# Low parts of the second and third masked pair: minus the high part from ScalarE and an accumulating transfer, in place of VectorE's difference

## The reference

```
top_p, top_i = top_k(softmax(gelu(xf @ w_r1 + b_r1) @ w_r2 + b_r2), 2); top_p /= sum(top_p)
for _ in range(2):
    ctx = concat(integrated, v)                                  # (2048, 256)
    shared_ctrl = gelu(ctx @ w_s1 + b_s1) @ w_s2 + b_s2
    x_shared, v_shared = inl(shared_ctrl, integrated, v, mu)
    hidden = gelu(ctx_e @ expert_w1[top_i] + expert_b1[top_i])   # 64 per chosen expert
    ctrl = hidden @ expert_w2[top_i] + expert_b2[top_i]          # 3 * 128: alpha, beta, gate
    x_r, v_r = weighted sum over the two experts of inl(ctrl, x_e, v_e, mu)
    x_next, v_next = sw * x_shared + (1 - sw) * x_r, sw * v_shared + (1 - sw) * v_r
    halt = sigmoid(gelu(x_next @ w_h1 + b_h1) @ w_h2 + b_h2)
    refined = gelu(x_next @ w_f1 + b_f1) @ w_f2 + b_f2
    integrated, v = integrated + halt * refined * integration_weight, v_next
```

## Time and profile before

| | |
|---|---|
| median of three runs | 358.88 us |
| the profiled execution | 360.02 us |
| its span | 358.2 us, 4385 instructions |
| TensorE | 327.9 us busy (92%), 1513 matmuls |
| VectorE | 284.2 us (79%) |
| ScalarE | 196.2 us (55%) |
| GpSimd | 21.1 us (6%) |
| chain that ended last | 70% TensorE, 19% VectorE, 3% ScalarE, 3% GpSimd, 2% DMA, 4% issue |

### The profile page before, as it was taken

How to read it: one execution, slowest core, us unless ns; L and a number is a source line. 1 busy time by engine, 2 the same in 40 slices (tenths; PEclk the granted TensorE clock), 3 DMA queues, 4 the chain that set the end, 5 groups by cost and what they waited for, 6 DMA issues and landing times.

```text
span 358.2 us, 4385 instructions
## 1 busy us (share of the span) xinstructions
PE 327.9 (92%) x1513; PEld 231.5 (65%) x1521; DVE 284.2 (79%) x598; ACT 196.2 (55%) x309; POOL 21.1 (6%) x24
## 2 busy tenths in 40 slices
PE   4989999899888889599798999999999999999996
PEld 4754787445454557367476677777777777777663
DVE  0556767655768777979997999999997997999694
ACT  2500025385637285186876686775855846734744
POOL 0040020202010112000000100000000000000000
PEclk9989999999999999789899999999999999999999
DMA  7999920000000000000000010100100100000001
GB/s 248 425 424 298 333 124 0 0 4 0 0 0 2 1 0 2 0 0 3 1 0 2 5 24 0 31 0 2 30 0 3 29 0 2 29 0 0 31 0 59
DMA packets 11445, 18.92 MB, mean 53 GB/s; under 512 B 416, under 2 KB 8864, under 8 KB 10144
## 3 DMA queue, kind: packets, MB, share of 16 engines
q1 hardware_dynamic: 10848, 17.60, 14.3%
q0 software_dynamic: 576, 1.05, 1.7%
HBM read 16.55 MB, written 1.05 MB: 49 GB/s over the span
## 4 chain that ended last, share of the span: by engine, by line
PE 70%; DVE 19%; issue 4%; ACT 3%; POOL 3%; DMA 2%; SPq 0%; DVEq 0%; ACTq 0%; POOLq 0%
PE ps L1200 65%; DVE zz L803 4%; POOL lrs L359 3%; DVE lst L788 2%; DMA ctxT<-in_ctxT 2%; PE ps L1297 1%; PE ps L1383 1%; PE ps L1276 1%; DVE lmv L791 1%; DVE st L688 1%; ACT hid L484 1%; PE ps L1371 1%; DVE a L704 1%; DVE lve L793 1%; DVE ctxT L1090 0%
## 5 line engine op out<-in xcount | busy, mean ns | idle before, releaser
L1200 PE MATMUL ps<-hm_odd,ew_hi 128*128 128x512 f32 (+1 forms) x164 | 52.3, 421 | 0.0
L1200 PE MATMUL ps<-hm_even,ew_hi 128*128 128x512 f32 (+1 forms) x160 | 49.7, 414 | 0.0
L1200 PEld LDWEIGHTS ps<-hm_odd,ew_hi 128*128 128x128 f32 (+1 forms) x164 | 29.1, 191 | 6.5 <-issue 0.5
L1200 PEld LDWEIGHTS ps<-hm_even,ew_hi 128*128 128x128 f32 (+1 forms) x160 | 27.5, 188 | 5.2
L1200 PE MATMUL ps<-hm_odd,ew_lo 128*128 128x512 f32 (+1 forms) x80 | 28.8, 397 | 0.0
L1200 PE MATMUL ps<-hm_even,ew_lo 128*128 128x512 f32 (+1 forms) x80 | 28.0, 390 | 0.0
L484 ACT ACTIVATE hid<-ps,pB 128x512 f32<-128x512 f32 x32 | 21.7, 687 | 10.4 <-PE ps L1200 9.7
L1200 PE MATMUL ps<-x_hi,w1x_hi 128*128 128x512 f32 x40 | 20.1, 503 | 5.7 <-ACT hid L484 3.9
L803 DVE TENSOR_SCALAR zz<-ps,lmv,lrs 128x128 f32<-128x128 f32 x48 | 16.4, 405 | 7.7 <-POOL lrs L359 7.5
L897 DVE SCALAR_TENSOR_TENSOR ring<-ring,pB,hid 128x1024 f32<-128x1024 bf16 x16 | 20.5, 1283 | 0.9
L788 DVE BATCH_NORM_STATS2 lst<-ps 128x6 f32<-128x128 f32 x48 | 10.7, 285 | 11.9 <-PE ps L1276 11.8
(11 more groups left out here) (286 smaller groups left out, 740.0 us busy)
## 6 DMA issues: line engine op xcount, KB each, us to landing
ring<-in_fc1b SPq DMA_DIRECT2D x4, 1024.0 KB, 17.8
ring<-in_fc2a SPq DMA_DIRECT2D x4, 1024.0 KB, 9.0
packC<-in_packC SPq DMA_DIRECT2D x1, 1152.0 KB, 9.2
pB<-in_packB SPq DMA_DIRECT2D x1, 1141.5 KB, 10.1
ctxT<-in_ctxT SPq DMA_DIRECT2D x2, 512.0 KB, 6.6
xtok<-in_xtok SPq DMA_DIRECT2D x1, 1024.0 KB, 9.2
xT<-in_xT SPq DMA_DIRECT2D x1, 1024.0 KB, 11.2
a<-in_fc1a SPq DMA_DIRECT2D x1, 1024.0 KB, 13.2
```

The source lines that it names most:

```text
L1200: return pe.matmul(out, lhsT, rhs, start=start, stop=stop)
```

## The change

VectorE keeps the masks and the high parts of all pairs, and the low part of tile 0 and of pair 1. For pairs 2 and 3, ScalarE writes minus `hm` to the low half, which as an fp32r value is minus the high part (`negative_high`), and GpSimd issues a transfer that adds `hm` to it in place (`low_part`, 512 KB). The semaphores `nhi` (ScalarE's copy) and `hlo_2`, `hlo_3` (the transfers) are new; the next masks wait on the transfers where they waited on the difference. In the BETA groups the three matmuls of each tile of pairs 2 and 3 are split in order: first high parts, at the end low parts. GpSimd's two loops are merged into one sequence.

```diff
             for n in range(3 * NCH):
+                power(n)
+            low_part(0, 2)
+            low_part(0, 3)
+            for s in range(1, STEPS):
+                if 3 <= s < NCH + 3:
+                    residual(s - 3)
+                low_part(s, 2)
+                low_part(s, 3)
...
+            def low_part(s, j):
+                pool.wait_ge(sem("nhi"), 2 * s + j - 1)
+                if s >= 1:
+                    pool.wait_ge(sem(f"hlo_{j}"), 16 * s)
+                pool.dma_start(low_of(s, j), hm[j % 2], accum_op=ALU.add).then_inc(sem(f"hlo_{j}"), 16)
...
+            def negative_high(s, j):
+                act.wait_ge(sem("hm"), (HT - 1) * s + j)
+                act.activation(low_of(s, j), hm[j % 2], ACT.Copy, scale=-1.0).then_inc(sem("nhi"), 1)
...
+            negative_high(0, 2)
+            negative_high(0, 3)
             act.wait_ge(sem("consts"), 4)
             for s in range(STEPS):
...
                 if s >= 1:
                     halt1(s - 1)
+                if s + 1 < STEPS:
+                    negative_high(s + 1, 2)
+                    negative_high(s + 1, 3)
                 squashed(s, parts(s)[1])
...
@@ kept(s, j)
-                if s >= 1 or j == 3:
-                    dve.wait_ge(sem("hlo"), HT * s + (0, -1, 2)[j - 1])
+                    if s >= 2:
+                        dve.wait_ge(sem("part_ps"), group(s - 1, 0))
+                if j == 3:
+                    dve.wait_ge(sem("hlo"), 2 * s + 2)
+                elif s >= 1:
+                    dve.wait_ge(sem("hlo_2" if j == 2 else "hlo_3"), 16 * s)
...
@@ hidden_masked(s, next_state)
                 lower(s, 0)
+                high(s, 1)
                 lower(s, 1)
                 kept(s, 3)
-                lower(s, 2)
+                high(s, 2)
                 shared_halves(s)
-                lower(s, 3)
+                high(s, 3)
...
@@ controls
-                    pe.wait_ge(sem("hlo"), HT * s + j + 1)
-                    out = hi if k else lo
-                    mm(out, weights(ew2_hi, j), m[:, 0, i, :], start=rows_last and j == 1, stop=False)
-                    mm(out, weights(ew2_lo, j), m[:, 0, i, :], start=False, stop=False)
-                    last = mm(out, weights(ew2_hi, j), m[:, 1, i, :], start=False,
-                              stop=not rows_last and j == HT - 1)
+                    high(i)
+                    if not rows_last or i < 3:
+                        last = low(i)
+                if rows_last:
+                    for i in range(3, NT):
+                        low(i)
```

More of the change, by code:

```diff
@@ L302, in masked, with high_of, low_of @@
             return hm_odd if s % 2 else hm_even
+        def high_of(s, j):
+            return masked(s)[:, 0, 2 * j - 1:2 * j + 1, :]
+        def low_of(s, j):
+            return masked(s)[:, 1, 2 * j - 1:2 * j + 1, :]
         SLOTS = NCH + 2
@@ L355, in _, with power @@
             pool.wait_ge(sem("r1one"), 1)
-            for n in range(3 * NCH):
+            def power(n):
                 pool.wait_ge(sem("lve"), n + 1)
@@ L360, in _, with residual @@
                     .then_inc(sem("lrs"), 1)
-            for s in range(NCH):
+            def low_part(s, j):
[3 more added lines that the diff above has]
+                pool.dma_start(low_of(s, j), hm[j % 2], accum_op=ALU.add).then_inc(sem(f"hlo_{j}"), 16)
+            def residual(s):
                 pool.wait_ge(sem("xi"), s + 1)
                 pool.dma_start(xT[:, ck(s)], xi[:, ck(s)], accum_op=ALU.add).then_inc(sem(f"xsum_{s}"), 16)
+            for n in range(3 * NCH):
+                power(n)
[6 more added lines that the diff above has]
+                low_part(s, 3)
         @block.scalar
@@ L473, in hidden_gelus @@
                         if s >= 1:
-                            act.wait_ge(sem("hm") if j else sem("hlo"), (HT - 1) * (s - 1) + j if j else HT * (s - 1) + 1)
+                            act.wait_ge(sem("hm") if j else sem("hlo"), (HT - 1) * (s - 1) + j if j else 2 * s - 1)
                         if j == 0:
@@ L899, in kept, with high @@
                                          ALU.is_equal, ALU.mult).then_inc(sem("hm"), 1)
+            def high(s, j):
+                dve.wait_ge(sem("hm"), (HT - 1) * s + j)
+                dve.tensor_copy(high_of(s, j), hm[j % 2]).then_inc(sem("hhi"), 1)
             def lower(s, j):
@@ L906, in lower @@
                     dve.wait_ge(sem("hhi_0"), s + 1)
[L907 to L915, removed]
+                    dve.tensor_tensor(out[:, 1, 0, :], hid[:, 0, :], out[:, 0, 0, :].bitcast(F), ALU.subtract)\
                         .then_inc(sem("hlo"), 1)
                 else:
-                    dve.tensor_tensor(out[:, 1, 0, :], hid[:, 0, :], out[:, 0, 0, :].bitcast(F), ALU.subtract)\
+                    dve.wait_ge(sem("hhi"), (HT - 1) * s + 1)
+                    dve.tensor_tensor(low_of(s, 1), hm[1], high_of(s, 1).bitcast(F), ALU.subtract)\
                         .then_inc(sem("hlo"), 1)
@@ L1053, in _ @@
             kept(0, 2)
+            high(0, 1)
             lower(0, 1)
@@ L1056, in _ @@
             state_split(1)
-            lower(0, 2)
+            high(0, 2)
             shared_halves(0)
-            lower(0, 3)
+            high(0, 3)
             route(NCH - 1)
@@ L1525, in weights, with high, low @@
                     return w[:, j * 3 * D + part * D:j * 3 * D + (part + 1) * D]
+                def high(i):
+                    j, k = TILES[i]
+                    pe.wait_ge(sem("hhi"), (HT - 1) * s + j)
+                    mm((lo, hi)[k], weights(ew2_hi, j), m[:, 0, i, :], start=rows_last and j == 1, stop=False)
+                    mm((lo, hi)[k], weights(ew2_lo, j), m[:, 0, i, :], start=False, stop=False)
+                def low(i):
+                    j, k = TILES[i]
+                    if j == 1:
+                        pe.wait_ge(sem("hlo"), 2 * s + 2)
+                    else:
+                        pe.wait_ge(sem(f"hlo_{j}"), 16 * (s + 1))
+                    last = mm((lo, hi)[k], weights(ew2_hi, j), m[:, 1, i, :], start=False,
+                              stop=not rows_last and j == HT - 1)
+                    if n == LAST and j == HT - 1:
+                        last.then_inc(sem("stream_ps"), 1)
+                    return last
                 def shared(first):
@@ L1536, in row_tiles @@
                     pe.wait_ge(sem("hsl"), s + 1)
-                    pe.wait_ge(sem("hlo"), HT * s + 1)
+                    pe.wait_ge(sem("hlo"), 2 * s + 1)
                     w_hi, w_lo = weights(ew2_hi, 0), weights(ew2_lo, 0)
@@ L1556, in controls @@
                 for i in (1, 3, 5, 2, 4, 6) if n == LAST else range(1, NT):
-                    j, k = TILES[i]
                     if i == 4 and between:
                         between()
-                    pe.wait_ge(sem("hlo"), HT * s + j + 1)
-                    out = hi if k else lo
-                    mm(out, weights(ew2_hi, j), m[:, 0, i, :], start=rows_last and j == 1, stop=False)
-                    mm(out, weights(ew2_lo, j), m[:, 0, i, :], start=False, stop=False)
-                    last = mm(out, weights(ew2_hi, j), m[:, 1, i, :], start=False,
-                              stop=not rows_last and j == HT - 1)
-                    if n == LAST and j == HT - 1:
-                        last.then_inc(sem("stream_ps"), 1)
+                    high(i)
[4 more added lines that the diff above has]
+                        low(i)
                 if rows_last:
```

## The result

The changed kernel takes 364.23 us (median of 4 runs, 363.83 to 364.61) where the kernel before takes 359.34 beside it (4 runs, 358.85 to 359.83). The ratio is 1.0136, 95% interval [1.0114, 1.0158]: slower by 4.9 us. The forecast was 362.5 in a range of 360.2 to 365.2, from a delay of 3.6.

The account below looks back on a forecast made before the run. TensorE was taken to bound the kernel from 197.6 to 331.7 us, with earlier waits on ScalarE's gelus. +1.80 + 2.76 - 0.94 = +3.6 us on the median 358.88 gave 362.5 us, range 360.2 to 365.2.

Parts of the forecast that it names:

- The bound: From 197.6 to 331.7 us TensorE is busy 134.07 of 134.10 us; time off VectorE there buys nothing by itself.
- Price of a copy, and the places: A 128x1024 ScalarE copy costs 0.95 us; between last gelu and GATE's tanh calls, delay reaches TensorE in four places.
- Step 0: Two copies ahead of the table load delay GATE's tanh, the gelu and TensorE's `hidden(2)` by 1.80 us.
- `hidden(3)`: TensorE's wait for ScalarE's gelu, 1.28 us, comes 0.92 later with the copies, to about 2.2.
- `hidden(4)` and `hidden(5)`: Copies behind the halt gelu delay GATE's tanh by 0.92 us each; TensorE's waits there come to about 1.1.
- The end: Step 7: without two VectorE subtractions, TensorE's wait before `refine_a(6)` goes whole, -0.94 us.
- The order, GpSimd and the transfers: BETA low parts last, sixteen GpSimd issues, 512 KB transfers landing in 5.1 us: all covered, no cost.
- the rival on late landings: Step 0's transfers at 7.4 us each in series make TensorE wait 2.9 us: 365.4 and above; chance 0.07.
- The clock: Rival: a second clock fall, behind the 2.2 us wait in `hidden(3)`, adds 1.6 us: 364.1; chance 0.20.
- The first fall: Behind the `hidden(2)` wait the clock fell to 0.53 for 3.3 us, about 1.6 lost; no change counted.
- The sum: Step 0, steps 1 to 3 and the end: +1.80 + 2.76 - 0.94 = +3.6 us.
- its two terms: Top of the range, 365.2: clock fall, +1.6 us, and dear copies at 1.02 each, +0.6, together.

Follow-up runs that it names:

- Steps 1 to 3 alone: Copies and transfers only for the masks of steps 2 to 4, copied in ScalarE's steps 1 to 3, against the kernel before: 362.30 us, 1.0075.
- Split places: Whole change, one copy ahead of the halt gelus and one behind, step 0's both ahead of the weights' copies, against the kernel before: 358.98 us, 0.9989.
- second part alone: Copies and transfers only for the masks of steps 5 to 7, the others by VectorE's difference, against the kernel before: 358.16 us, 0.9973.
- order: All differences on VectorE, only the change's order of BETA matmuls and its mask waits, against the kernel before: 358.93 us, 0.9990.
- step 0 alone: Copies and transfers only for the masks of step 1, copied in ScalarE's step 0, against the kernel before: 361.97 us, 1.0066.
- first part alone: Copies and transfers only for the masks of steps 0 to 4, VectorE's difference for 5 to 7, against the kernel before: 364.77 us, 1.0166.
- filler: Extra matmuls into a free bank at the start of the `hidden(2)` wait: ten in the kernel before, 0.9978; eighteen in the change, 1.0099 to the kernel before.

## Why the prediction was right, and which term was short

- **The bound.** TensorE sets the pace from 197 us on, and time off VectorE buys nothing there: right. Without any of the differences of six steps the kernel gains 1.2 us, all but a little of it the one wait at the end.
- **Price of a copy, and the places.** 0.95 us from start to start was forecast and measured. Step 0 in the trace: +1.79 for 1.80. `hidden(3)`: +0.88 for 0.92. `hidden(4)` and `hidden(5)`: +0.81 and +0.83, and waits of 0.77 where 1.1 was forecast. There the tanh did move by 0.90, but some 0.1 came back right behind it: L484 used to start 2.15 us after the tanh, now 2.04. The gelu ahead of it (L482) started at 215.63 in the trace of before, 0.04 after the end of the last matmul that it needs; the copies have moved it well behind that. Steps 1 to 3 alone cost 2.7 us on the clock of the runs, with 2.76 forecast. Split places shows that the mechanism is the place and not the copy.
- **The end.** -0.94 forecast; -0.97 in the traces, and -0.97 with the second part alone. That L1097 waits next for the tanh, and that this still leaves the whole wait, held.
- **The order, GpSimd and the transfers.** Priced at nothing, and no TensorE wait ends on a transfer: right within the intervals (order 0.9990; transfers at most 0.0017). The landings are 4.5 to 6.7 us: the pair-2 ones near the 5.1 taken, those of pair 3, which start 0.9 us behind, 6.1 and 6.2 (median). That is past the 5.9 from which the rival on late landings was to decide, but that rival had the two in series at 7.4 each; they run side by side and land within 8 us of the first issue. One statement here was wrong: "The new waits of `kept` on the transfers are met 5 us or more ahead". In step 1 the mask on VectorE waits 2.31 us for the pair-3 transfer of step 0, up to 157.48. No cost of it shows: TensorE works from 155.66 on without a gap.
- **The clock.** This is the term that was shown to be short, for 0.6 of the 1.3 us missing, in the rival's sentence "The first fall may also come out shorter, as more of it is spent waiting; I count nothing". It came out longer: 6.7 us low instead of 3.4. Step 0's copies cost 2.4 us instead of 1.80, and the traces of the change and of step 0 alone gain 0.5 behind the wait, where the clock is low. The size is not fixed: in the first part alone the same wait of 4.43 gives a shorter fall, with 16.9 us where the change has 17.5. The rival itself, a second fall behind the 2.2 us wait, came in one of the five traces that have that wait, the one of steps 1 to 3 alone, and cost 1.4 there; that the prediction left it out of its sum and gave it a chance was sound. Its price of 1.6 a fall doesn't follow from its own count: nine matmuls instead of fourteen, at 0.23 each, are some 1.2 us, and the traces give 1.3. What holds in place of "I count nothing": a delay that lengthens an idle stretch of the array is to be priced with the fall behind it, at either size, and as a thing that comes in some executions only.
- **The sum.** +2.4, +2.7 and -0.97 make 4.1 of the 4.9 measured, forecast 3.6. The other 0.8 isn't settled. It has the size by which the first part alone exceeds its two halves, and lies within the intervals. A second fall of 1.4 us in some of the executions could give as much, but the one trace of the change has none, and no run tests it.

The measured delay of 4.9 lies nearer to the 5.2 of the clock's rival than to the 3.6 of the forecast; the mechanism of the forecast carries most of it, and the rest is that rival's kind of cost in part and open in part. The range's top of 365.2 is 0.5 above what its two terms give (362.5 + 1.6 + 0.6 = 364.7); the measured 364.23 lies below both. And the forecast in time, 362.5 for 364.23, is off by 0.5 more than that in the delay, as the kernel before, 358.88 in the first three runs, was 359.34 beside the changed one.

## What to carry to other kernels

Before moving work to an engine with idle time, look up in its timeline what stands behind the place and who waits for that: with the sixteen copies at one place the kernel lost 4.9 us, and with half of the copies put ahead of the two instructions that stood before them it lost nothing. Look for the gap of the right size on each side of the instructions that others wait for, and put there what fits. A relief counts only where the relieved engine is waited for, so the change is worth making for three steps of eight at most (0.9973).

## What the runs showed of the hardware

**GpSimd's issue of a transfer can be held by a VectorE cast.** In the trace of after, GpSimd's first two issues of the low parts, the third, and the casts of VectorE beside the first two:

```profile
149.70 1.35 POOL L375 DMA_DIRECT2D hm_even<-wz  x1 [6.34 <-ACT hm_even L569]
150.63 1.86 POOL L375 DMA_DIRECT2D hm_even<-ring  x1
169.77 0.87 POOL L375 DMA_DIRECT2D hm_odd<-wz  x1 [17.28 <-ACT hm_odd L569]
```

```profile
150.19 0.77 DVE L944 CAST hm_even<-wz 128x1024 fp32r<-128x1024 f32 x1
150.99 0.69 DVE L992 TENSOR_TENSOR hsh<-wz,hsh 64x512 fp32r<-64x512 f32 x1
151.71 0.69 DVE L944 CAST hm_even<-ring 128x1024 fp32r<-128x1024 f32 x1
```

The other fourteen issues take 0.87 us; these took 1.35 and 1.86, each running until 0.09 us after the end of a cast (151.05 and 150.96, 152.49 and 152.40), and the cast of 150.19 took 0.77 instead of 0.69. Not all of the excess is the casts'. In the kernel with step 0's copies alone the first two issues stand beside no cast:

```profile
169.77 1.05 POOL L387 DMA_DIRECT2D hm_odd<-wz  x1 [26.44 <-ACT hm_odd L583]
170.72 1.02 POOL L387 DMA_DIRECT2D hm_odd<-ring  x1
```

So some 0.3 and 0.8 us are left for the casts. Split places shows it once more on an issue that is not the first, GpSimd and then the cast of VectorE:

```profile
166.44 1.33 POOL L375 DMA_DIRECT2D hm_odd<-wz  x1 [14.44 <-ACT hm_odd L569]
```

```profile
167.00 0.68 DVE L947 CAST hm_odd<-wz 128x1024 fp32r<-128x1024 f32 x1
```

In the traces of four kernels all seven issues that had a 128x1024 cast begin 0.49 to 1.08 us behind their start ended 0.08 to 0.09 after that cast. The prediction held from one row that casts don't hold an issue; the cast of that row ended 0.22 us after the issue began. The rule that it set against this (the Trainium skill, "SBUF — State Buffer", section "SBUF: two separate sides") agrees with these rows: a VectorE copy in its two-port mode and GpSimd take one port in turns. The hold cost no time. The one wait of VectorE on such a transfer, 2.31 us in the change, is as long or longer (2.43 and 2.45) in three kernels where the second issue took 1.41 instead of 1.86, so it is the transfer's landing and not the hold:

```profile
157.48 1.28 DVE L937 SCALAR_TENSOR_TENSOR ring<-ring,pB,hid 128x1024 f32<-128x1024 bf16 x1 [2.31 <-DMA hm_even<-ring]
```

**The clock's falls differ between executions of the same code.** Up to 162 us the kernel with the copies of steps 1 to 3 alone runs the same instructions as the kernel before, but for the order of some matmuls from 157 us on. The first line is of before, the two below of that kernel:

```profile
140.00:162.00 22.00, 17.30 (x69) 12.06 (x70) 19.45 (x49) 10.60 (x16) 1.98 (x1) 0.84 0.00 0
```

```profile
140.00:162.00 22.00, 18.95 (x69) 13.06 (x69) 19.45 (x50) 10.59 (x16) 1.98 (x1) 0.77 0.00 0
162.00:192.00 30.00, 27.27 (x140) 20.44 (x139) 28.11 (x33) 22.62 (x32) 0.00 (x0) 1.00 0.01 2
```

0.84 and 0.77 are 7.0 and 10.1 us at the lower level. The second execution, with the same wait of 2.65 us in `hidden(2)`, then has no fall behind it, where the kernel before had one. Over the traces of all kernels here, a fall came behind waits of 2.65 to 2.76 without filler in four of six, behind waits of 4.43 without filler in four of four, behind waits of 2.16 in one of five, and behind waits of 1.28 in none of seven. So a single trace can be off by a microsecond in either stretch, and a term of half a microsecond for the clock is read from medians, not from one pair of traces.
